# A two-layer gated cross-attention block with expert layers on one core: the product with the values in one run, the masked layer in steps of two chunks

## The reference

```
x = x + tanh(g_xattn[0]) * differential_attention(norm(x), ctx)      # layer 0: 32 score heads of 4 features, 16 value heads of 8
x = x + tanh(g_ffn[0])   * top2_experts_with_shared_expert(norm(x))
x = x + tanh(g_xattn[1]) * masked_attention(norm(x), ctx, mask)      # layer 1: 16 heads of 8 features
x = x + tanh(g_ffn[1])   * top2_gated_experts(norm(x))

scores = einsum('bhqd,bhkd->bhqk', q, k) * scale                     # 56 x 1500 for each head and batch
scores = where(mask, finfo.min, scores)                              # layer 1 alone
out    = einsum('bhqk,bhkd->bhqd', softmax(scores), v)
```

## Time and profile before

| | us |
|---|---|
| median of three runs | 2355.09 |
| lowest and highest | 2350.68, 2356.16 |
| the profiled execution, its own time | 2361.65 |
| its span, first to last instruction | 2359.2 |
| PE busy | 2192.7 (93%) |
| DVE busy | 1677.1 (71%) |
| ACT busy | 1507.8 (64%) |
| POOL busy | 1278.9 (54%) |
| mean granted TensorE clock | 0.946 |

### The profile page before, as it was taken

The page is one execution under the profiler, slowest core; times in us unless marked ns, Lnnn a source line. Parts: engine busy times, 40 slices in busy tenths (PEclk is TensorE's granted clock), DMA queues, the critical chain, the costliest instruction groups (busy, mean ns, idle before and its releaser), DMA issues. The chain is left out here.

```text
span 2359.2 us, 67435 instructions
## 1 busy us (share of the span) xinstructions
PE 2192.7 (93%) x27256; PEld 1303.0 (55%) x27256; DVE 1677.1 (71%) x3697; ACT 1507.8 (64%) x2133; POOL 1278.9 (54%) x1418
## 2 busy tenths in 40 slices
PE   4799999999999999999967957999999999999798
PEld 3255555555555555555536843666655666666576
DVE  3688888888888888888816555777766677774644
ACT  2177788777877778778763322767666667766322
POOL 5335655655654554655333445777766777762232
PEclk8599999999999999999997975999999999999699
DMA  3635344344444444444201027667665666661100
GB/s 105 128 77 113 96 98 109 101 94 108 106 97 99 112 96 95 115 93 94 48 7 57 24 61 149 137 142 137 143 131 120 127 144 140 138 126 24 54 1 16
DMA packets 113421, 227.82 MB, mean 97 GB/s; under 512 B 46052, under 2 KB 58596, under 8 KB 112612
## 3 DMA queue, kind: packets, MB, share of 16 engines
q1 hardware_dynamic: 113124, 223.67, 42.8%
HBM read 146.77 MB, written 76.48 MB: 95 GB/s over the span
## 5 line engine op out<-in xcount | busy, mean ns | idle before, releaser
L1061 ACT ACTIVATE probs<-score_ps 125x896 f32<-125x896 f32 x1152 | 1014.3, 915 | 210.3 <-PE score_ps L954 207.9
L1119 DVE TENSOR_REDUCE max_part<-max_ps 112x1 f32<-112x500 f32 x1024 | 654.7, 668 | 115.3 <-PE spare_ps L923 68.3
L970 PE MATMUL acc_ps<-probs,vext 125*32 125x224 f32 (+1 forms) x12288 | 673.2, 316 | 6.6 <-issue 6.1
L923 PE MATMUL max_ps<-kstack,qstack 48*112 48x500 f16 x1535 | 508.1, 405 | 4.9 <-DVE max_part L1119 2.6
L954 PE MATMUL score_ps<-qstack,kstack 50*125 50x224 f16 (+1 forms) x6144 | 454.8, 244 | 17.2 <-ACT probs L1061 13.9
L954 PEld LDWEIGHTS score_ps<-qstack,kstack 50*125 50x125 f16 x6144 | 344.4, 134 | 183.8 <-issue 122.2
L1116 DVE CUSTOM_DVE_ANT_0 kstack<-max_ps,kstack 112x500 f32<-112x500 f32 x511 | 335.3, 675 | 134.2 <-PE max_ps L923 80.1
L1119 DVE TENSOR_REDUCE max_part<-spare_ps 112x1 f32<-112x500 f32 x512 | 343.3, 670 | 64.6 <-PE max_ps L923 63.5
L970 PEld LDWEIGHTS acc_ps<-probs,vext 125*32 125x32 f32 x12288 | 261.7, 109 | 225.8 <-issue 156.5
L923 PE MATMUL spare_ps<-kstack,qstack 48*112 48x500 f16 x769 | 310.7, 404 | 20.2 <-issue 16.9
L923 PEld LDWEIGHTS max_ps<-kstack,qstack 48*112 48x112 f16 x1535 | 173.5, 129 | 143.4 <-issue 77.7
(11 more groups left out here) (200 smaller groups left out, 2697.8 us busy)
## 6 DMA issues: line engine op xcount, KB each, us to landing
kstack<-k_parts SPq DMA_DIRECT2D x384, 187.5 KB, 6.6
k_parts<-khl SPq DMA_DIRECT2D x128, 375.0 KB, 2.8
ctx_f<-in_ctx SPq DMA_DIRECT2D x32, 750.0 KB
ctx_f<-context_parts SPq DMA_DIRECT2D x32, 750.0 KB, 4.4
context_parts<-ctx_f SPq DMA_DIRECT2D x16, 750.0 KB, 3.8
context_parts<-kstack SPq DMA_DIRECT2D x16, 750.0 KB, 3.5
mask_in<-in_mask SPq DMA_DIRECT2D x128, 82.0 KB
qrows<-q_parts SPq DMA_DIRECT2D x384, 7.0 KB, 7.0
```

Of the source, the lines that this page charges most:

```text
L923: nc.tensor.matmul(room(("P", n, p))[0:PIECE, 0:TK], qstack[n % SLOTS][rows, c, PIECE * i:PIECE * (i + 1)], kstack[n % SLOTS][rows, c, TK ...
L970: last = nc.tensor.matmul(acc_ps[32 * j:32 * j + 32, TT * S * i:TT * S * (i + 1)].rearrange("p (s c) -> p s c", s=S), vext[n % SLOTS][:, t ...
L1061: nc.scalar.activation(probs[t % 2][:, 896 * h:896 * h + 896].rearrange("k (b c) -> k b c", b=2), score_ps[(t * H + h) % 2][0:KT, :, 0:448 ...
L1119: nc.vector.reduce_max(best, scores, AX.X).then_inc(s_red, 1)
```

## The change

Three things change in `attend`. (1) `weigh` makes all 8 matmuls of a chunk in one run. (2) A step of layer 1 now holds two chunks, so that it has 6 steps (`STEPS`), each with scores place 0 and 1, two search pairs, one run of 16 product matmuls and the preparations of `where`, which now use the place-0 score bank as in layer 0; F is one use of four turns instead of two of two; `AHEAD` is 3 of 6 steps. The order in a step is chosen by `order_of` from whether this step and the one before have preparations other than A and M. (3) On SP the next context load of layer 1 stands behind `fill_m`; on POOL the additive mask is converted ahead of the other one, and without the wait between them.

```diff
@@ Layer
-        self.uses_f = 2
+        self.uses_f = self.halves
+        self.steps = NKT if self.halves == 2 else NKT // 2
@@ attend
-    GD, GC, H = L.group_dims, L.group_cols, L.halves
+    GD, GC, H, STEPS = L.group_dims, L.group_cols, L.halves, L.steps
...
     else:
-        where = {("V", 0): (0, 2), ("F", 0): (1, 2), ("V", 1): (2, 2), ("F", 1): (3, 2), ("V", 2): (4, 2), ("K", 0): (5, 2),
-                 ("K", 1): (6, 2), ("M", 0): (7, 2), ("K", 2): (8, 2), ("A", 0): (10, 2)}
+        where = {("F", 0): (1, 1), ("V", 0): (1, 0), ("V", 1): (2, 0), ("V", 2): (2, 1), ("M", 0): (3, 1), ("K", 0): (3, 0),
+                 ("K", 1): (4, 0), ("K", 2): (4, 1), ("A", 0): (5, 1)}
         keyed = [("K", i) for i in range(NTHIRD)]
     valued = [("V", i) for i in range(NTHIRD)]
-    per_step = L.pieces // NKT
-    assert per_step * NKT == L.pieces
-    AHEAD = 5
+    per_step = L.pieces // STEPS
+    assert per_step * STEPS == L.pieces
+    AHEAD = 3 if L.masked else 5
     early = AHEAD * per_step
+    ORDERS = {"both scores first": ("scores 0", "scores 1", "pair 0", "weigh", "pair 1", "prepare"),
+              "scores apart by a pair": ("scores 0", "pair 0", "scores 1", "weigh", "pair 1", "prepare"),
+              "scores apart by the product": ("scores 0", "pair 0", "weigh", "scores 1", "pair 1", "prepare"),
+              "pairs apart by preparation": ("scores 0", "weigh", "scores 1", "pair 0", "prepare", "pair 1")}
+
+    def order_of(n, t):
+
+        busy = [any(kind not in "AM" for kind, _, _ in at_step(*place)) for place in ((n, t), (n, t - 1) if t else (n - 1, STEPS - 1))]
+        if not busy[1]:
+            return ORDERS["both scores first"]
+        if L.masked and not busy[0]:
+            return ORDERS["scores apart by a pair"]
+        return ORDERS["scores apart by the product" if L.masked and busy[0] else "scores apart by the product" if busy[0] else "scores apart by the product"]
...
     def searched(n, t, k):
-        if 2 * k >= per_step:
-            return []
-        d, place = (1, early + t * per_step) if t < NKT - AHEAD else (2, (t - NKT + AHEAD) * per_step)
+        d, place = (1, early + t * per_step) if t < STEPS - AHEAD else (2, (t - STEPS + AHEAD) * per_step)
...
         if user in in_scores:
-            return score_ps[halves_of(in_scores[user])[0]][:, int(user[0] in "MA"), :]
+            return score_ps[halves_of(in_scores[user])[0]][:, where[user[0], user[2]][1], :]
...
             def next_mask(n):
                 if L.masked:
                     sp.wait_ge(s_add, n)
+                    sp.wait_ge(s_big, n)
                     load_mask(sp, T, L, n)
...
                 if n + 3 < B:
                     load_q(n + 3)
                     next_mask(n + 3)
-                    if L.masked:
-                        next_context(n + 4)
...
                 if n + 1 < B:
                     fill_m(n + 1)
                 if n + 3 < B:
+                    if L.masked:
+                        next_context(n + 4)
                     store_k(n + 3)
...
+                    nc.gpsimd.tensor_scalar(by_chunk(mask_add[n % SLOTS]), turned_keys(T["mask_in2"][:, :]),
+                                            -BIG * BIG, None, ALU.mult).then_inc(s_add, 1)
                     nc.gpsimd.tensor_scalar(by_chunk(mask_f[n % SLOTS][0:HALF + SQ, :]), turned_keys(mask_in[0:HALF + SQ, :]),
                                             -BIG, None, ALU.mult).then_inc(s_big, 1)
-                    pool.wait_ge(s_big, n + 1)
-                    nc.gpsimd.tensor_scalar(by_chunk(mask_add[n % SLOTS]), turned_keys(T["mask_in2"][:, :]),
-                                            -BIG * BIG, None, ALU.mult).then_inc(s_add, 1)
...
             def scores(n, t, place):
-                if L.masked:
-                    at_least(pe, s_exp, number - 1)
-                elif place == 0:
+                if place == 0:
                     at_least(pe, s_exp, number)
                 else:
                     at_least(pe, s_exp, number - 2)
...
-                buf = score_ps[(t * H + h) % 2]
-                keys = slice(KT * t, KT * t + KT)
+                buf = score_ps[h]
+                chunk, columns = (t, range(h * 2, h * 2 + 2)) if H == 2 else (2 * t + h, range(PAIRS))
+                keys = slice(KT * chunk, KT * chunk + KT)
...
+            def weigh(n, t):
+                pe.wait_ge(s_exp, (n * STEPS + t + 1) * 2)
+                if t == 0:
+                    at_least(pe, s_os, n)
+                    pe.wait_ge(s_v, NTHIRD * (n + 1))
+                chunks = [(t, 0)] if H == 2 else [(2 * t + h, 896 * h) for h in range(2)]
+                for chunk, column in chunks:
+                    for i in range(2):
+                        for j in range(4):
...
             for n in range(B):
-                for t in range(NKT):
+                for t in range(STEPS):
                     weighed = (n, t - 1) if t else (n - 1, LAST)
-                    scores(n, t, 0)
-                    search(searched(n, t, 0))
-                    if H == 2:
-                        scores(n, t, 1)
-                    for i in range(2):
-                        if i == 1 and (t or H == 1):
-                            search(searched(n, t, 1))
-                            for user in at_step(n, t, 1):
+                    for work in order_of(n, t):
+                        if work in ("scores 0", "scores 1"):
+                            scores(n, t, int(work[-1]))
+                        elif work in ("pair 0", "pair 1"):
+                            search(searched(n, t, int(work[-1])))
+                        elif work == "weigh" and weighed[0] >= 0:
+                            weigh(*weighed)
+                        elif work == "prepare":
+                            for user in at_step(n, t):
                                 use(user)
-                        if weighed[0] >= 0:
-                            weigh(*weighed, i)
```

More of the change, by code:

```diff
@@ L606, in halves_of @@
     def halves_of(step):
-        return (0, 1) if step % 2 == 0 or H == 1 else (1, 0)
+        return (0, 1) if step % 2 == 0 else (1, 0)
     def room(user):
@@ L949, in scores @@
                                          big_eye[HALF * r:HALF * r + SQ, :], start=True, stop=False, skip_group_check=True)
-                here = PAIRS // H
-                for k in range(here):
+                for k, c in enumerate(columns):
                     for r in range(2):
                         rows = slice(HALF * r, HALF * r + KROWS + 2)
-                        last = nc.tensor.matmul(buf[0:KT, r, GC * k:GC * (k + 1)], kstack[n % SLOTS][rows, h * here + k, keys],
-                                                qstack[n % SLOTS][rows, h * here + k, :], start=not L.masked, stop=True,
+                        last = nc.tensor.matmul(buf[0:KT, r, GC * k:GC * (k + 1)], kstack[n % SLOTS][rows, c, keys],
+                                                qstack[n % SLOTS][rows, c, :], start=not L.masked, stop=True,
@@ L1150, in _ @@
             for n in range(B):
[L1151 removed]
+                for t in range(STEPS):
                     for user in searched(n, t, 0):
                         reduce_piece(user)
[L1154 to L1156 removed]
+                    if t == where["F", L.uses_f - 1][0] + 1 and n:
                         reciprocals(n)
```

98 lines of the change are left out of this document (40 added, 58 removed).

## The result

| | before | after |
|---|---|---|
| median of the runs, us | 2355.39 (4 runs) | 2422.17 (4 runs) |
| lowest and highest | 2350.68, 2356.16 | 2410.58, 2424.02 |
| ratio, 95% interval | | 1.0277 [1.0243, 1.0312] |
| the profiled execution, its span | 2361.65, 2359.2 | 2424.02, 2422.2 |
| mean granted clock | 0.946 | 0.918 |

I had forecast 2316 us. The page of the changed kernel shows where to look: busy tenths in 40 slices of 60.6 us, and the granted clock in tenths. The full batches of layer 0 lie in slices 3 to 19, the loop of layer 1 in slices 25 to 37.

A forecast was written before the change was run, and what follows sets the result against it. PE bounds both loops; after the change, layer 0's exponentials and layer 1's keys loop would. Layer 0 -27, layer 1 -14, tail +2 make -39 on 2361.65, 2322.7; the median is 6.6 lower: 2316 us, range 2272 to 2350.

The forecast's parts named there:

- The chain of exponentials: Layer 0: scores wait for the exponential of the step before, which sets steps of 2.85 us, batches of 34.1, -27 us.
- (c): Exponentials' chain 0.1 us longer than read: layer 0 gains nothing, layer 1 its 14 us; 2343 us; chance 0.12.
- (d): The product in one run does not save the turns; layer 0 batch 35.7 us; 2371 us in all; chance 0.05.
- The tail of +2: Last two batches of layer 1, without preparations: steps wait for both their exponentials, +2 us in all.
- The context's delay of nothing: Layer 1: context load issued just ahead of the keys' store could make it 1.7 us late (term +33); no delay taken.
- PE's 20.5 in layer 1: Layer 1: PE's own work summed step by step, 20.5 us a batch instead of 22.32.
- the loads' 9.9 us: Layer 1: the six stacked-key loads keep the DMA engines busy 9.9 us, and the search waits for all six.
- my own loop: Layer 1: search's first piece to last third of keys, store, loads and back: 6.0 + 4.89 + 1.0 + 9.9 = 21.8 us.
- rival (b): Clock falls in layer 1 after the stall of 1.3 us in each batch: 24.8 us a batch, 2400 us; chance 0.13.
- The old loop: Layer 1 before the change, the keys' loop: 2.8 + 4.89 + 9.9 = 17.6 us, well inside the batch of 22.32.
- the same sort of gap, at full clock: Last batch of layer 0 before: a gap in each step, granted clock 1.00; so no clock term in layer 0.

The follow-up runs named there:

- the run with layer 0 alone: The kernel before, with scores apart by the product in all layer 0 steps but t = 1 and the product in one run; layer 1 as before: 2350.03 us, 0.9992.
- the paced kernel: The kernel before with the changed kernel's layer 0; in layer 1 SP issues the last two stacked-key loads only when the first four have landed: 2315.78 us, 0.9839.
- the filler kernel: The changed kernel with 14 more search matmuls, results overwritten, ahead of the wait for the stacked-key loads in each layer 1 batch: 2396.49 us, 1.0169.

## Why the prediction was wrong

- **Layer 0 was right.** 34.1 forecast, 34.11 measured (from 35.01 that is 0.9, where I took 0.95). The chain of exponentials sets the steps as summed: in the changed kernel

```profile
579.83 0.96 PE L979 MATMUL acc_ps<-probs,vext 125*32 125x224 f32 x16
...
580.72 0.41 PE L962 MATMUL score_ps<-qstack,kstack 50*125 50x224 f16 x4
...
581.17 0.92 ACT L1065 ACTIVATE probs<-score_ps 125x896 f32<-125x896 f32 x1 [0.53 <-PE score_ps L962]
...
582.14 0.41 PE L962 MATMUL score_ps<-qstack,kstack 50*125 50x224 f16 x4 [0.22 <-ACT probs L1065]
...
582.69 0.96 PE L979 MATMUL acc_ps<-probs,vext 125*32 125x224 f32 x16
```

  the product runs 0.89 us in the queue (579.83 to 580.72) and a step with T takes 582.69 - 579.83 = 2.86 where 2.85 was summed. Rivals (c) and (d) are out. A wait for ACT is listed 5 times in a batch (once 0.8 us, four times 0.2) and not in nearly every step: in those with K and V PE's own work is within 0.15 us of the chain. The 28 batches are worth 28 x 0.90 = 25 us; the last ones give 1 to 2 back (33.23, 28.95, 26.52, where they were 32.12, 28.81, 26.2), and the run with the old layer 1 and `order_of` in layer 0 shows 24.
- **The tail of +2 was luck.** 2.0 was measured, but the last two intervals between copies, of which the forecast spoke, are shorter than before (15.35 and 13.46, where they were 16.12 and 13.73). The 2.0 come from the batch ahead of them, which still waits for its loads (27.1, was 24.62).
- **The context's delay of nothing was right**, by the run with the context back.
- **PE's 20.5 in layer 1 was right:** 20.3 with four loads.
- **The step that failed is the loads' 9.9 us** in "the DMA engines are then busy for 20 slices, to 1713.4". I took the point where the busy share falls for the landing. Behind the nines of the earlier trace rows stands a tail ("1421"), and a search waits for the last landing of all six loads. The view of the six loads would have told it: the last is issued at 1706.7 and the slowest takes 7.8 us, so they are down by at most 1714.5, 11.1 us after the first.

```profile
L675 SPq DMA_DIRECT2D kstack<-k_parts x6: 303/426/812, 1703.4 to 1706.7; - x6
...
DMA to landing us min/median/max: 4.4/6.7/7.8
```

  In the changed kernel the waits end 10.7 to 12.2 us after the first load, mostly at 11.5. That is +1.6, and nothing that the change brought: in the kernel before they are down at 11.3 in the median. Store to first load has a median of 2.9 (+0.2). With these my own loop reads 6.0 + 5.1 + 1.0 + 11.5 = 23.6 us at full clock, and the wait 23.6 - 20.5 = 3.1, not 1.3.
- **The clock, as a consequence.** A stall of 3 us is beyond the 1.98 of the earlier trace rows, so rival (b), 0.13, is what came, in each batch. It had 24.8 us a batch and 2400 in all; measured were 25.92 and 2422. Against the forecast's 21.8, 1.8 are the longer loop (23.6) and 2.3 slow matmuls. That is a feedback that I didn't sum: the slow matmuls stand between the search's first piece and the last third of the keys, inside the loop, so that they lengthen the wait of the batch after too. My sum held the clock and the loop as separate cases, while one sets off the other; the run with the later search gives 1.2 us of slow matmuls back for 1.65 of loop. (The old loop adds up to 2.3 + 4.89 + 9.9 = 17.1 and not 17.6; with either it was far inside the batch.)
- **Chances.** The forecast had the loads as a single row to 0.1 us, while 1.4 us more a batch (39 / 28) took the whole gain. 0.13 was too little for (b).

On the rule that was weighed: the Trainium skill ("TensorE: Matmul & The Clock Gate", "A second HAM failure mode: psum-queue depth-cycling") has small idle times between groups swing the clock. In the full batches of layer 0 this case doesn't bear it out: 140 recorded waits for ACT, 48.6 us in all and none over 0.8, and a clock of 1.00.

```profile
PE score_ps L962 <- ACT probs L1065: 48.6, 140, 0.8
```

In the run with layer 0 alone it does bear it out: after four steps with waits for ACT of 0.8 us, and during one of 1.0, the clock fell at 1170.1 for 20.5 us. So "the same sort of gap, at full clock", from which the prediction gave the term nothing, held for layer 0 in the trace of the change, and not for steps whose waits were little longer. (The run with `order_of` in layer 0 has 3.4 us at the lower level at 1190.4, in its last batches.) In layer 1 the clock does swing, after waits of 1 to 4 us for a DMA.

**What stays open.** That the "issue" stalls are waits for instructions is borne out by the packets behind whose ends they end; that the fetches are late because of the queued loads, by the paced kernel. A fetch was never moved or removed by itself, and a long one need not stall PE: of the 24 of over 1.5 us above only four did. Which place in the program it hits, and so why some batches of the same kernel are free of it, wasn't tried.

## What to carry to other kernels

Where a change moves a producer later and its consumer earlier, sum the whole loop (consumer's place to producer's, store, loads, back) and hold it against the new length of the batch, not the old. Take the end of a group of loads from the landing of the slowest, not from where the DMA share falls. A wait that comes out at 2 us or more should be priced with the slow matmuls behind it, and these again with the loop in which they stand. A sum that holds a wait to be harmless because it is shorter needs a run: here waits of 0.8 us went either way.

## What the runs showed of the hardware

- Idle PE is dearer than busy PE: 3 us of useless matmuls in each batch, ahead of a wait, made the kernel 26 us faster.
- How a queue is filled tells on an engine that doesn't use it: 65 of 68 stalls without a shown releaser end 1.2 to 1.8 us after the end of a 16 KB instruction packet. With six loads at once PE stands now and then for 1.7 to 2.9 us in the middle of a group (23 to 27 us for a batch); with four and then two each batch is 22.31.
- In the change and the kernel with the later search a wait of 1.0 to 1.3 us left the clock alone in 6 of 8 cases, one over 2.5 us in none of 30. That is no threshold: in the filler kernel 8 of 18 waits under 1 us came with a low stretch, and in layer 0 with the scores apart waits of 0.8 us in each step did.
